# Two graph layers on one core: the store of x1 is issued ahead of SP's wait for the scatter's last chunk, in phase B

## What is computed

```python
h = jnp.maximum(_layernorm(x, axis=-1), 0.0)
x = x + _L0_gnn_ref(h, L0_gnn_W_l, L0_gnn_W_r, edge_index)   # mean over a node's edges, two products
h = jnp.maximum(_layernorm(x, axis=-1), 0.0)
x = x + _L1_gnn_ref(h, edge_index, edge_attr_128, ...)
# _L1_gnn_ref:
agg = jax.ops.segment_sum(edge_attr, src, num_segments=x.shape[0])
h = jnp.concatenate([x, agg], axis=1)
h = _bn(jax.nn.silu(h @ W1 + b1), g1, be1)
h = _bn(jax.nn.silu(h @ W2 + b2), g2, be2)
return h @ W3 + b3
```

## Time and profile before

| | us |
|---|---|
| median of three runs | 1533.28 |
| the profiled execution, its own time | 1530.96 |
| span of the profiled execution | 1529.2 |
| phase B, first scatter (661.9) to last landing (1163.7) | 501.8 |
| busy in the span: PE, DVE, ACT, POOL | 1062.3, 1101.3, 868.1, 836.9 |

### The profile page before, as it was taken

One profiled execution on the slowest core, in us unless ns is written; L12 is line 12 of the kernel. 1 busy time (PEld: TensorE's weight loads), 2 busy tenths in 40 slices (PEclk: granted clock), 3 DMA queues, 4 the chain that ended last, 5 costly groups with the idle time before them and its releaser, 6 DMA issues.

```text
span 1529.2 us, 23466 instructions
## 1 busy us (share of the span) xinstructions
PE 1062.3 (69%) x5247; PEld 746.2 (49%) x5247; DVE 1101.3 (72%) x4641; ACT 868.1 (57%) x1686; POOL 836.9 (55%) x601
## 2 busy tenths in 40 slices
PE   3656776776656666637777777666666877997866
PEld 1235555665544444524444444444444765446765
DVE  6987777776556555538888888776753877778978
ACT  5956566656544544327666766655563545665533
POOL 6768888888888888657666667665652000000000
PEclk9989989889888978769999999998986998998989
DMA  9979889877666666557887778899986996306999
GB/s 278 386 250 225 218 216 216 192 163 159 146 146 146 145 145 143 120 137 188 194 197 192 194 193 201 238 259 257 265 231 198 354 326 229 136 27 235 407 403 372
DMA packets 231506, 333.62 MB, mean 218 GB/s; under 512 B 42106, under 2 KB 93394, under 8 KB 231444
## 3 DMA queue, kind: packets, MB, share of 16 engines
q1 hardware_dynamic: 157516, 285.22, 55.6%
q0 software_dynamic: 68864, 38.50, 20.3%
q10 hardware_dynamic: 5064, 9.29, 1.9%
HBM read 179.16 MB, written 153.71 MB: 218 GB/s over the span
## 4 chain that ended last, share of the span: by engine, by line
POOL 36%; DMA 26%; issue 15%; PE 12%; DVE 8%; SPq 1%; ACT 1%; DVEq 1%; POOLq 0%; ACTq 0%
POOL acc L808 20%; POOL acc L824 10%; DMA acc<-tabs,target_b 8%; DMA acc<-zT,target_b 8%; POOL xin L785 6%; PE ps L1494 6%; DMA zT<-x_dram 3%; DVE res L1088 2%; DMA xin<-acc 2%; PE ps L1504 2%; PE ps L1470 1%; PE ps L1473 1%; DVE zT L1342 1%; DVE zT L1346 1%; PE ps L1476 1%
## 5 line engine op out<-in xcount | busy, mean ns | idle before, releaser
L1390 PE MATMUL ps<-zT 128*128 128x512 f32 (+5 forms) x784 | 298.7, 536 | 206.7 <-ACT zT L924 133.2
L808 POOL DMA_INDIRECT acc<-zT,tabs x196 | 316.7, 1616 | 69.2 <-issue 58.5
L1390 PEld LDWEIGHTS ps<-zT 128*128 128x128 f32 (+1 forms) x784 | 172.7, 231 | 358.8 <-issue 197.4
L877 ACT ACTIVATE zT<-res,zT 128x128 f32<-128x128 f32 x398 | 158.5, 480 | 111.4 <-DVE zT L1167 111.4
L824 POOL DMA_INDIRECT acc<-zT,target_b x100 | 163.9, 1639 | 91.8 <-DMA acc<-tabs,target_b 30.5
L1125 DVE SCALAR_TENSOR_TENSOR zT<-zT 128x128 f32<-128x128 f32 (+3 forms) x392 | 193.2, 549 | 11.7 <-DMA zT<-row_dram 5.4
L824 POOL DMA_INDIRECT acc<-tabs,target_b x96 | 152.1, 1584 | 90.3 <-DMA acc<-tabs,target_b 31.2
L1193 DVE BATCH_NORM_STATS2 zT<-zT 128x6 f32<-128x128 f32 (+1 forms) x384 | 79.2, 279 | 164.8 <-DMA zT<-in_x_dram 164.5
L785 POOL DMA_INDIRECT xin<-in_x_dram,tabs x140 | 144.3, 1031 | 53.5 <-issue 42.1
L1382 PE MATMUL ps<-ident,zT 128*128 128x128 f32 (+1 forms) x784 | 118.4, 300 | 62.4 <-ACT zT L877 62.2
L1419 PE MATMUL ps<-wr,hT 128*128 128x128 f32 (+1 forms) x784 | 103.0, 286 | 53.2 <-DVE zT L1184 48.9
(11 more groups left out here) (148 smaller groups left out, 1959.7 us busy)
## 6 DMA issues: line engine op xcount, KB each, us to landing
acc<-bst SPq DMA_DIRECT2D x12, 2112.0 KB, 21.9
acc<-bst SPq DMA_DIRECT2D x48, 528.0 KB
zT<-row_dram SPq DMA_DIRECT2D x98, 256.0 KB, 5.6
zT<-in_x_dram SPq DMA_DIRECT2D x48, 512.0 KB, 6.8
zT<-acc SPq DMA_DIRECT2D x48, 512.0 KB, 4.3
x_dram<-res SPq DMA_DIRECT2D x48, 512.0 KB, 5.2
zT<-x_dram SPq DMA_DIRECT2D x42, 512.0 KB, 8.6
out_dram<-zT SPq DMA_DIRECT2D x42, 512.0 KB, 7.9
```

The source lines that it names most:

```text
L808: pool.indirect_dma_start(acc1, bass.IndirectOffsetOnAxis(ap=target_a[0:p, k, j:j + 1], axis=0), v[0:p, j, :], None, compute_op=ALU.add).t ...
L877: ins = nc.scalar.activation(to[0:p, c, :], t[0:p, c, :], ACT.Identity, bias=nm[0:p, par, k:k + 1], scale=rs[0:p, par, k:k + 1])
L1390: ins = nc.tensor.matmul(psA[:, 0:j + 1, 0:p], t[0:p, j, :], same[0:p, par, at:at + j + 1, 0:p], start=(j == ROWS - 1), stop=(j == 0))
```

## The change

In `step_b` SP waits for x1 of the round and stores it first; the wait for chunk 3's landing comes behind that, then the node loads and the edge loads.

```diff
             def step_b(before, now, after, ahead):
 
                 i, par, tail, spill, _ = now
+                sp.wait_ge(*this(B["added"], par, i))
+                store_nodes(res[:, par, :, :], x1_v, 2 * i + par, tail, B["stored"][par])
                 sp.wait_ge(*this(s_end2, par, i, 16))
                 if ahead:
                     load_b_nodes(*ahead)
-                sp.wait_ge(*this(B["added"], par, i))
-                store_nodes(res[:, par, :, :], x1_v, 2 * i + par, tail, B["stored"][par])
                 if type(i) is not int or 2 * (i + 2) + par <= RF:
                     load_b_edges(i + 2, par, type(i) is int and i + 2 == IT, 0)
```

## The result

The changed kernel takes 1557.03 us, the median of four runs (1553.7 to 1558.21), the kernel before beside it 1533.53 us (four runs). The ratio is 1.0152, its 95% interval 1.0134 to 1.017: slower by 23.5 us. The direction was forecast, the size not: 5.2 us were, and the range ended at 1546.

What follows compares the result with a forecast made beforehand. B was taken as bound by chunk 2's landings, a round being burst, scatter and hole. Terms 7 (z stores) - 2.7 (end) + 0.9 (start) = +5.2 us on 1533.3 gave 1538.5 us, range 1526 to 1546.

Steps and rivals of the forecast that it cites:

- What bounds B: Phase B: the chain runs between landings of chunk 2; a round is the burst's bytes, the scatter's, then a packetless hole.
- the prediction's own sign: Phase B before round 32: a change of more than 0.15 us a round would show the reading of the queues wrong.
- its reading of the queues: DMA queues in B: SP's burst moves first, GpSimd's scatter after it, then no packet moves until SP's next burst.
- The store becomes the last of the same burst: SP's queue in B's steady rounds: node loads, names, edges, then round k+1's store; same bytes, none in the hole.
- Its price of 0: Moved store in 31 rounds before round 32: costs 0, with 0.12 us a round, 4 us in all, allowed either side.
- slower already before round 32: Rival: burst-end store writes and scatter adds hinder each other in DRAM, 0.3 us in 31 rounds, +9 us; chance 0.08.
- VectorE and z come earlier: From round 32 on, VectorE no longer waits for the store, so VectorE, ScalarE and the z store come 1.8 us earlier.
- +0.5 a round, +7 us: Some 14 rounds from round 32 on: earlier z stores cost at the scatter, bounds +10.5 and -7.7 us.
- The end of B, -2.7 us: Last store issued before the last scatter lands, so phase C's first load goes at about 1163.9 instead of 1166.62.
- The start, +0.9: Start of B: round 1's store, issued beside chunk 2 of round 1, costs 0.9 us, bounds 0 and 1.3.
- Nothing but the two ends: Rival: the moved z store costs at the scatter what it saves at the next burst's start; 1531.5 us, chance 0.30.
- freed burst: Rival: earlier z no longer runs into the burst's start, all rounds from 32 cheap; 1523.8 us, half 1527.6; chance 0.22.

Runs made afterwards that it cites:

- e4: Kernel before, but round k+1's store issued at chunk 2's landing, then node loads, names, attributes behind chunk 3's landing; ratio 0.9818.
- e12: As e4 (store of round k+1 at chunk 2's landing), but loads ordered node loads, attributes, names; 1507.24 us, ratio 0.9843 to the kernel before.
- e13: As e12 without SP's wait for chunk 3: store and loads all issued at chunk 2's landing; 1506.00 us, ratio 0.9832 to the kernel before.
- e5: The change with its edge loads split and reordered: node loads, attributes, store of round k+1, names; ratio 0.9973 to the kernel before.
- e6: The change with the burst reordered: node loads, names, store of round k+1, attributes; ratio 1.0071 to the kernel before.
- e10: The change with ScalarE's z store issued behind the round's relu instead of behind the copy of z; ratio 1.0074 to the kernel before.
- e1: Kernel before, with round k+1's store in place of round k's, second in the burst (node loads, store, names, attributes); ratio 0.9986.
- f1: The change with names and attributes exchanged: node loads, attributes, names, store of round k+1; ratio 1.0015 to the kernel before.
- e9: As e5, with the attribute load reading one row of names for all partitions (sums not those asked for); ratio 0.9979 to the kernel before.
- e7: The change with round k+1's store first in the burst, then node loads, names, attributes, all behind chunk 3's landing; ratio 0.9925 to the kernel before.

## Why the prediction was right or wrong

**What bounds B: right in the main.** The chain still runs over the flights of chunk 2, and e4, e12 and e13, built on burst, scatter and hole, won 1.6 to 1.8%. But by the prediction's own sign (rounds before 32 changing by more than 0.15 us) its reading of the queues failed, with 0.21: it took the burst's time as given by its bytes.

**The store becomes the last of the same burst: right. Its price of 0: wrong.** This is the first step that failed, "The bytes are the same ... Price in 31 rounds before round 32: 0", with 4 us allowed. It measured 6.2 us in 29 rounds, 0.21 us each. The rival "slower already before round 32" (0.3 us each) was nearer, but had the wrong place: I looked for hindrance where the scatter's packets meet the store's, and the engines move too little in the middle of the burst, 3.5 to 4.5 us behind its start. The same bytes in another order are not the same time. e5 and e6, which exchange two loads of equal size, differ by 0.23 us a round.

**VectorE and z come earlier: right. What that costs: wrong in size and in reason.** The step was "Some 14 rounds ... +0.5 a round, +7 us". 17.9 us in 15 rounds were measured, of which e10 assigns at least 0.85 x 15 = 13 us to z's place. The remaining 5 us (e10 against the kernel before: 11.43 and 11.09) are of the order, or of the z stores that e10 left early; no run tells which. Two things failed in it. The forecast moved z by 1.8 us against a landing that it held fixed; but z hangs on the node loads of a step before, the landing on the current burst. When a round gets longer, z comes earlier within it. Against the step before, z moved by 2.4 us (20.9 to 18.5), not far from the forecast's 1.8; against its own step it moved by 3.8 us (9.9 to 6.2), since the round grew as well. And the price was put at the wrong place: about 2.3 us ahead of the landing is free (e1, on average), 5.3 us ahead, as with the change, is dear. There z's packets go ahead of the scatter's last, and the hole, which they filled before, is left empty. By this reading the dip pushes the rounds into a place where z collides, and the collision lengthens them further. f1 fits that: with the dip partly filled z is issued 7.3 us behind the node loads and the round takes 11.10 us. That the two feed each other is argued from these rows, not shown by a run of its own.

**The end of B, -2.7 us: right,** though the two rounds before it gave back 3.1. **The start, +0.9: not seen,** chunk 0 of round 3 is issued at 700.55 and 700.49.

**The rivals.** "Nothing but the two ends" and "freed burst" did not come about with the change; but the latter's mechanism did in e1 and e5. There z lies early, all rounds are cheap, and they take 10.84 and 10.85 us, 0.25 us a round less than before. With the store second in the burst this rival holds; with the store last it does not. The rule of the Trainium skill (DMA: Bandwidth & Descriptors, Queues, rings and completion order) that each engine takes the queues with work in turns would have had z's packets go soon after 1044.14; a z store on quiet engines has its first packet 0.84 us behind the issue. The trace has them from about 1047.5 on, though GpSimd's queue moved 121 packets between 1045.1 and 1047.1. So here too the trace does not bear the rule out, and the measurement decides; what held z's packets no run shows.

## What to carry to other kernels

When DMA engines bound a loop, look for the time in which they move nothing, and ask of an edit whether it puts work there; issuing a transfer at another point of the same burst moves no work into it. A store issued one landing sooner, while the engines would otherwise wait for the next loads, was worth 1.8% here. And reckon the place of a transfer relative to the loop's period, not to a fixed clock: whatever lengthens the round moves every transfer that hangs on an earlier round's loads. Count the bytes that the engines move beside their busy share: in e6 the share hid the loss.

## What the runs showed of the hardware

- The order of four DMAs in one queue, with the same bytes, went with a change of a round by 0.1 to 0.2 us. With names ahead of the store the 16 engines moved 121 to 199 GB/s from 3.5 to 4.5 us behind the first load, with names behind it 270 to 382. With the change they were 72% busy there, in e6 full. Reading one row for all partitions is not the cause (e9).
- A burst that begins with a store to DRAM moves 182 packets in the second microsecond behind its issue, one that begins with a load from DRAM 65; on average over the rounds before 32 it is 181 in e7, 64 in the kernel before and 94 with the change.
- A DMA that ScalarE's queue issued into SP's burst had no packet until the burst thinned out: z was issued at 1044.14 and served from about 1047.5, 3.7 us behind its issue, against 0.84 us on quiet engines.
